# Scaling folded into the value weights, q and k split straight from PSUM, and one-hot lane products moved to ScalarE, in a fused attention and mixture-of-experts kernel

## The reference

```
# 1. self attention over the 1024 pixels of each image
q, k, v = Wq@xf + bq, Wk@xf + bk, Wv@xf + bv          # 32, 32 and 256 rows
y = v @ softmax(q.T @ k, axis=-1).T
x = alpha[0] * y + x
# 2. to tokens (4 x 1024 x 256); proxy attention on the layer norm, with a running sum
prods = proxy @ ln(t).T                               # 16 proxies
y = cumsum(prods[..., None] * ln(t)[:, None], axis=2)
t = t + einsum('bps,bpsd->bsd', softmax(prods / sqrt(16), axis=1), y)
# 3. mixture of 8 experts, top 2 of each token, 256 -> 1024 -> 256
logits = ln(t) @ gate_w.T
combine = one_hot(top2) * softmax(top2 logits)
t = t + sum over e of combine[:, e] * (gelu(ln(t) @ w1[e] + b1[e]) @ w2[e] + b2[e])
```

## Time and profile before

| | |
|---|---|
| time, median of 3 executions | 826.69 us (822.74 to 829.28) |
| the profiled execution | 822.62 us, its span 820.9 us |
| busy PE, DVE, ACT, POOL | 726.5, 500.5, 320.7, 415.4 us |
| mean granted TensorE clock | 0.958 of full speed |

### The profile page before, as it was taken

The page is one execution under the profiler, slowest core; times in us unless marked ns, Lnnn a source line. Parts: engine busy times, 40 slices in busy tenths (PEclk is TensorE's granted clock), DMA queues, the critical chain, the costliest instruction groups (busy, mean ns, idle before and its releaser), DMA issues.

```text
span 820.9 us, 18490 instructions
## 1 busy us (share of the span) xinstructions
PE 726.5 (88%) x5437; PEld 687.8 (84%) x5439; DVE 500.5 (61%) x1095; ACT 320.7 (39%) x608; POOL 415.4 (51%) x480
## 2 busy tenths in 40 slices
PE   5898998988958768637999999999999999999993
PEld 4897897978846556427999999999999999999993
DVE  3787787877774898892545554555545455545551
ACT  2663854735723545223332233223323332332230
POOL 1473574775554454346355564555546555545233
PEclk9999999999988899878999999999999999999998
DMA  7659477494552132222364752756555545554222
GB/s 246 220 196 419 148 269 300 154 326 187 205 206 78 53 105 85 72 79 67 97 188 143 255 150 41 248 154 174 188 177 154 141 144 160 140 145 144 27 28 28
DMA packets 45872, 130.14 MB, mean 159 GB/s; under 512 B 5184, under 2 KB 35520, under 8 KB 41216
## 3 DMA queue, kind: packets, MB, share of 16 engines
q1 hardware_dynamic: 30560, 104.86, 34.1%
q0 software_dynamic: 13904, 19.45, 14.1%
q10 hardware_dynamic: 1360, 5.24, 1.6%
HBM read 186.80 MB, written 47.59 MB: 286 GB/s over the span
## 4 chain that ended last, share of the span: by engine, by line
PE 52%; issue 1%; DMA 1%; POOL 1%; DVE 0%; POOLq 0%; ACT 0%; DVEq 0%
PE ps_h L73 9%; PE ps_h L74 8%; PE ps_h L75 8%; PE ps_y L73 8%; PE ps_y L75 8%; PE ps_y L74 8%; PE ps_x L1585 2%; DMA out_tok<-y,to_row 0%; POOL out_tok L1460 0%; DMA x_rows<-normed,from_row 0%; POOLq L1383 0%; DVE yb L1540 0%; DVE xtl L1520 0%; DVE y L1547 0%; ACT xth L1485 0%
## 5 line engine op out<-in xcount | busy, mean ns | idle before, releaser
L1494 ACT ACTIVATE g<-ps_h,bias 128x256 f32<-128x256 f32 x288 | 120.9, 471 | 278.9 <-PE ps_h L75 278.8
L1460 POOL DMA_INDIRECT out_tok<-y,to_row x72 | 118.3, 1643 | 161.2 <-DVE y L1547 149.4
L73 PE MATMUL ps_h<-xth,wbuf 128*128 128x256 f32 x576 | 163.6, 284 | 3.3 <-issue 1.9
L73 PE MATMUL ps_y<-wbuf,gl 128*128 x576 | 164.4, 285 | 0.0
L74 PE MATMUL ps_h<-xtl,wbuf 128*128 128x256 f32 x576 | 163.5, 284 | 0.0
L75 PE MATMUL ps_h<-xth,wbuf 128*128 128x256 f32 x576 | 162.4, 282 | 0.0
L75 PE MATMUL ps_y<-wbuf,gh 128*128 x576 | 161.4, 280 | 0.0
L74 PE MATMUL ps_y<-wbuf,gh 128*128 x576 | 161.4, 280 | 0.0
L73 PEld LDWEIGHTS ps_h<-xth,wbuf 128*128 128x128 f32 x576 | 108.7, 189 | 3.7 <-issue 2.1
L75 PEld LDWEIGHTS ps_h<-xth,wbuf 128*128 128x128 f32 x576 | 110.1, 191 | 0.0
L74 PEld LDWEIGHTS ps_h<-xtl,wbuf 128*128 128x128 f32 x576 | 108.9, 189 | 0.0
(11 more groups left out here) (239 smaller groups left out, 1391.5 us busy)
## 6 DMA issues: line engine op xcount, KB each, us to landing
wbuf<-wsplit SPq DMA_DIRECT2D x71, 2048.0 KB, 7.4
wsplit<-wbuf SPq DMA_DIRECT2D x14, 2048.0 KB, 11.9
wraw<-in_w SPq DMA_DIRECT2D x16, 1024.0 KB, 7.7
raw<-in_x_ch ACTq DMA_DIRECT2D x5, 1024.0 KB, 9.1
normed<-x SPq DMA_DIRECT2D x8, 528.0 KB, 3.0
tok<-in_x_tok SPq DMA_DIRECT2D x1, 4096.0 KB, 16.7
out_tok<-tok SPq DMA_DIRECT2D x8, 512.0 KB, 3.8
x_rows<-normed,from_row POOLq DMA_INDIRECT x72, 3.3
```

The lines of the kernel that those rows point to most:

```text
L73: eng.matmul(out, ll, rh, start=first, stop=False)
L1460: pool.indirect_dma_start(out=out, out_offset=bass.IndirectOffsetOnAxis(ap=to_row[:, par, s:s + 1], axis=0), in_=y[:, par, s, :], in_offse ...
L1494: last = act.activation(g[:, f, :], ps_h[:, q, f % 2, :], ACT.Gelu_apprx_tanh, bias=bias1[:, bass.ds(e, 1), f:f + 1].rearrange("p a f -> p ...
```

## The change

Alpha is multiplied once, at the start, into v's weights and bias, and the product with alpha for each tile (L558, 32 times) goes. ACT writes the high half of q and k directly from PSUM (`high_qk`), and DVE makes the low half in one instruction from PSUM, bias and high half (`low_qk`); the wait for the last scores of the image before moves to ACT. POOL's subtraction of 128x2048 becomes four of 128x512, with the semaphore on the fourth. In the softmax of the routing weights the subtraction (`relative`) and the last product (`whole_weights`) move from DVE to POOL, and the last image's tiles are cut into batches of 2 and 6 instead of 4 and 4. In stage B the product of lanes and tile number moves from POOL to four activations of 128x256 on ACT (`number_lanes`); POOL's `next_tile` waits for them before it counts up the tile number. PE's `record(i - 2)` stands behind `attend(i + 1)` and `turn(i + 2)`. Some settings to zero are reordered.

```diff
-REST = IT // 2
+EARLY = 2
+PIECES = 4
...
-BATCHES = ((0, NT - 2 * IT), (NT - 2 * IT, NT - IT), (NT - IT, NT - REST), (NT - REST, NT))
+BATCHES = ((0, NT - 2 * IT), (NT - 2 * IT, NT - IT), (NT - IT, NT - IT + EARLY), (NT - IT + EARLY, NT))
...
+    def relative(self, pool, lo, hi, n):
+
+        pool.wait_ge(self.inv_step, n * 6 + 6)
+        pool.wait_ge(self.top_d, n + 1)
+        pool.tensor_tensor(self.weights[:, lo:hi, :], self.t[:, lo:hi, C:C + NP],
+                           self.top[:, lo:hi].unsqueeze(2).to_broadcast([P, hi - lo, NP]), ALU.subtract).then_inc(self.rel_d, 1)
...
+                        if not more and (par, part) == (1, 0):
+                            tok.relative(pool, *BATCHES[2], 2)
...
-                        pool.tensor_tensor(wbuf[:, par, at + n:at + 2 * n], wraw[:, part],
-                                           wbuf[:, par, at:at + n].bitcast(F32), ALU.subtract).then_inc(w_lo, 1)
+                        m = n // PIECES
+                        for i in range(PIECES):
+                            last = pool.tensor_tensor(wbuf[:, par, at + n + i * m:at + n + (i + 1) * m],
...
+                        last.then_inc(w_lo, 1)
...
-            def whole_qk(b, kind):
+            def high_qk(b, kind):
                 act.wait_ge(qk_mm, done(b * 2 + kind))
-                act.wait_ge(turned, done(b * IT - 2 + kind))
-                act.activation(qkf[:, kind], (ps_sc, ps_pt[0])[kind][0:3 * MID, :], ACT.Identity,
-                               bias=bqk[:, kind:kind + 1]).then_inc(qk_full, 1)
+                act.wait_ge(scored, done(b * IT - 1))
+                act.activation(qk3[:, kind], (ps_sc, ps_pt[0])[kind][0:3 * MID, :], ACT.Identity,
+                               bias=bqk[:, kind:kind + 1]).then_inc(qk_hi, 1)
...
-                dve.tensor_copy(qk3[:, kind], qkf[:, kind]).then_inc(qk_hi, 1)
+            def low_qk(b, kind):
+
+                at = slice(MID, 2 * MID) if kind == 0 else slice(2 * MID, 3 * MID)
                 dve.wait_ge(qk_hi, done(b * 2 + kind))
-                at = slice(MID, 2 * MID) if kind == 0 else slice(2 * MID, 3 * MID)
-                dve.tensor_tensor(qk3[at, kind], qkf[at, kind], qk3[at, kind].bitcast(F32), ALU.subtract).then_inc(qk_ok, 1)
+                dve.scalar_tensor_tensor(out=qk3[at, kind], in0=(ps_sc, ps_pt[0])[kind][at, :], scalar=bqk[at, kind:kind + 1],
+                                         in1=qk3[at, kind].bitcast(F32), op0=ALU.add, op1=ALU.subtract).then_inc(qk_ok, 1)
...
-                    dve.tensor_tensor(scale[:, col], scale[:, col], alb[:, :], ALU.mult).then_inc(scaled, 1)
-                    dve.wait_ge(scaled, done(g))
...
-            def lanes_by_tile(c, par):
+            def next_tile(c):
...
+                act.wait_ge(tile_d, done(c - 1))
+                mine = lane[:, :, :].rearrange("p (k b) l -> p b k l", k=2)
+                for b in range(B):
+                    last = act.activation(lane_tile[:, par].rearrange("p (k b) l -> p b k l", k=2)[:, b], mine[:, b], ACT.Copy,
+                                          scale=tile_no[:, b:b + 1])
+                last.then_inc(lane_tile_d, 1)
...
-                if exists(i - 2):
-                    record(i - 2, par)
                 if exists(i + 1):
                     attend(i + 1, 1 - par)
                 if exists(i + 2):
                     turn(i + 2)
+                if exists(i - 2):
+                    record(i - 2, par)
```

More of the change, by code:

```diff
@@ L352, in image @@
                                        ALU.subtract).then_inc(v_ok, 1)
+                static = isinstance(b, int)
+                if not more:
+                    tok.relative(pool, *BATCHES[0], 0)
                 for par in range(2):
@@ L372, in _ @@
         def _(act):
-            for s in (exped, pt_hi, qk_full, v_hi):
+            for s in (exped, pt_hi, qk_hi, v_hi):
                 act.sem_inc(s, CREDIT)
@@ L432, in image @@
                         exp_tile(it + 2)
-                    if not more and it in (REST, IT - 2):
-                        n = 1 + it // (IT - 2)
-                        tok.exponential(act, *BATCHES[n], n)
+                    if not more and it == 1:
+                        tok.exponential(act, *BATCHES[0], 0)
+                    if not more and it == IT - 2:
+                        for n in (1, 2):
+                            tok.exponential(act, *BATCHES[n], n)
                     if it == 2 and more:
@@ L444, in image @@
                 if more:
-                    whole_qk(b + 1, 1)
-                if isinstance(b, int) and b == B - 2:
-                    tok.exponential(act, *BATCHES[0], 0)
+                    high_qk(b + 1, 1)
             load_x(0)
@@ L523, in routing_weights @@
                     if more and it == IT - 2:
-                        tok.softmax_in(dve, *BATCHES[0], 0)
+                        tok.largest(dve, *BATCHES[0], 0)
                     if not more and it == 0:
                         tok.mean_var(dve, *BATCHES[1], 1)
-                        tok.softmax_out(dve, *BATCHES[0], 0)
-                    if not more and it == REST - 1:
-                        tok.softmax_in(dve, *BATCHES[1], 1)
-                    if not more and it == REST:
+                    if not more and it == EARLY:
                         tok.mean_var(dve, *BATCHES[2], 2)
-                    if not more and it == REST + 1:
-                        tok.softmax_out(dve, *BATCHES[1], 1)
-                    if not more and it == IT - 2:
-                        tok.softmax_in(dve, *BATCHES[2], 2)
+                        tok.sums_of_weights(dve, *BATCHES[0], 0)
+                    if not more and it in (3, 5):
+                        n = it // 2
+                        tok.largest(dve, *BATCHES[n], n)
                     if not more and it == IT - 1:
-                        tok.softmax_out(dve, *BATCHES[2], 2)
+                        for n in (1, 2):
+                            tok.sums_of_weights(dve, *BATCHES[n], n)
                 full_v(0)
@@ L894, in body @@
                 if exists(i - 1):
-                    lanes_by_tile(i - 1, 1 - par)
+                    next_tile(i - 1)
             pool.memset(prod_in[:, :, :], 0.0)
@@ L919, in _ @@
             tok.products(pool, fixed, *BATCHES[LAST], LAST)
-            for i in range(-1, 2):
+            body(-1, 1)
+            tok.relative(pool, *BATCHES[LAST], LAST)
+            tok.whole_weights(pool, *BATCHES[LAST], LAST)
+            for i in range(0, 2):
                 body(i, i % 2)
@@ L955, in evacuate_turned, with number_lanes @@
                 last.then_inc(turned_d, 1)
-            def lanes_by_part(c, par):
+            def number_lanes(c, par):
                 act.wait_ge(lane_d, done(c))
@@ L973, in body @@
                 if exists(i - 1):
-                    lanes_by_part(i - 1, 1 - par)
+                    number_lanes(i - 1, 1 - par)
             act.wait_ge(zeroed, 2)
```

101 lines of the change are left out of this document (49 added, 52 removed).

## The result

The changed kernel takes 784.75 us in the median of 4 runs (782.13 to 785.98), against 824.88 us for the kernel before (822.74 to 829.28, 4 runs): a ratio of 0.950, 95% interval 0.945 to 0.955. The forecast for the median was 794.0, the range 779 to 812. The profiled execution took 782.13 us, with a span of 780.4 against 820.9: 40.5 us less, where the sum in the prediction was 32.7.

A forecast was written before the change was run, and what follows sets the result against it. DVE instructions stalled behind long POOL ones, making PE wait in stage A, and the longest ring of engine steps in stage B were taken as bounds; 15.7 + 17.0 = 32.7 us gained, forecast median 794.0 us, range 779 to 812.

The forecast's parts named there:

- Start: Stage A, first image: only an unblocked cast goes, 0.7 of the 1.50 us that PE waits for first scores.
- Image changes: Stage A, three later images: PE's waits for first scores vanish, 8.6 us, and shorter pipeline refills give 3.0 more.
- The refill: Stage A, first scores to first sums after image changes: falls to the first image's 10.18 us, gaining 3.0 together.
- The rival in which the waits stay: Stage A's image changes: ACT's high half queues behind other work, PE waits as before, the 8.6 stay; 803 us, chance 0.07.
- The last image: End of stage A: 3.4 us gained, bounds 1.4 and 5.5, limited by POOL's wait ahead of its last eight pieces.
- the "more is gained" rival: DVE's 9.8 us sets stage B's chunk (4 more) or the last image gives 8.4 (5 more): 785 to 790, chance 0.10.
- Stage B: Five chunks going from 13.39 to 10.6 us give 14.0, the last three chunks 3.0: 17.0 us, bounds 11 and 23.
- the longest ring sets the spacing of the cells: Stage B: of three rings of dependent engine steps, the longest sets the chunk's new period, taken as 10.6 us.
- The ring of ACT and POOL: Stage B chunk: ACT's busy time, four activations and POOL's stretch to ACT's next work make 10.5 us, taken as 10.6.
- its own ring: Stage B chunk on DVE: 13.46 us minus its 1.75 wait for ps_a and about 1.95 of cell stall leaves 9.8.
- The drain: Stage B's last three chunks, where the loop runs out: about 1.0 us gained in each, 3.0 together.
- TensorE's clock: Rival in stage B: PE's granted clock sinks to a mean of 0.6, five chunks lose 4.0 us; 812, chance 0.06.

The follow-up runs named there:

- the late step: Changed kernel with POOL's softmax subtraction of batch 2 between the last two groups of four weight pieces instead of ahead of both: 782.62 us.
- the spread weights: The late step's kernel with ACT's high halves of the weights made one per tile to the end, instead of two at tile 5: 779.94 us.

## Why the prediction was right, and where its sum was off

The direction, the places and most of the mechanisms held. The sum was 7.8 us too small, 3.3 of it in stage A, 3.4 in stage B and the rest outside both. The median, 784.75, lies 9.3 under the forecast; the other 1.5 is the distance from the profiled execution to the median, 2.6 where I added 4.1.

- *Start*, forecast 0.7: the wait fell from 1.50 to 0.84, as worked out. The first sum came 2.0 us earlier: 0.4 more because q's first matmul started at 12.31 instead of 12.71, and 0.9 more because fewer of q's matmuls ran at the lower clock, 0.63 us each (six, eleven before). Among the kernels with the new split, whose PE instructions up to there are the same, the first sum comes between 31.83 and 33.54, so this excess cannot be put down to the change.
- *Image changes*, forecast 8.6 + 3.0: the waits went in full, and the three images gave 13.5. The refill was under-sized, 4.0 for 3.0: from 10.89, 11.63 and 11.45 it falls to 10.05, 9.97 and 9.97, below the first image's 10.18, and the granted clock in these stretches, which was 0.85 and 0.86 at the last two changes before, is 1.00. The forecast of the refill had no term for the clock. The last 1.0 us lies inside the images. The rival in which the waits stay, 803, would have needed ACT to be late; ACT's high half came in time for PE at every change. Of the two causes that I named together, the split alone does it; the pieces are a second remedy for the same wait, and on the kernel before they leave most of it.
- *The last image*, forecast 3.4: 3.5 measured, by the mechanism named, POOL's wait ahead of the last eight pieces. The wait ended at 208.42 in a stage whose last image began 15.5 us earlier than before (at 180.98 against 196.48), so at 223.9 by the old clock, where I had 224.5. The 8.4 that the "more is gained" rival allowed was there to take: the late step and the spread weights take 4.4 more.
- *Stage B*, forecast 14.0 + 3.0: here a step failed, that the longest ring sets the spacing of the cells. The ring of ACT and POOL, for which I had 10.6, was sized nearly right: ACT's normalisations, released by POOL, follow at 10.19 to 10.56. But DVE's cells do not wait for it. Three of the five blocks follow at 9.88 or 9.89 and one at 9.99, with no wait of DVE: its own ring, which I had put at 9.8 and among the rivals at 0.10 (785 to 790; the median lies at its edge). ACT's lanes fall behind, from 0.12 to 1.26 us after the first cell, and catch up where the loop runs out. The remaining chunk takes 10.70, and its limit is PE, busy for all of it behind a chunk at a clock of 0.83; DVE waits 0.70 for `ps_out`. In the run with the weights spread the chunk ahead is at 1.00 and DVE waits nowhere. Whether the longer ring would set the pace of a longer loop, no run shows.

```profile
265.17:275.87 10.70, 10.70 (x62) 8.31 (x60) 9.80 (x58) 8.71 (x22) 4.98 (x19) 1.00 0.29 100
...
267.52 0.19 DVE L1025 TENSOR_TENSOR raw_logit<-ps_out,tok 128x32 f32<-128x32 f32 x1 [0.70 <-PE ps_out L1270]
...
270.80 2.08 ACT L944 ACTIVATE raw<-tok,inv_shift 128x256 f32 x4 [1.06 <-POOL inv_shift L847]
...
281.36 2.08 ACT L944 ACTIVATE raw<-tok,inv_shift 128x256 f32 x4 [1.12 <-POOL inv_shift L847]
...
291.54 2.08 ACT L944 ACTIVATE raw<-tok,inv_shift 128x256 f32 x4 [0.98 <-POOL inv_shift L847]
```

The terms: the four activations take 1.69, not 1.9, and from the lanes' end to ACT's next normalisation it is 2.08 to 2.46 us, where I had 2.2; eight free cells take 1.67, not 1.4. Five chunks gave 16.6. The drain and the table gave 3.9; I had 3.0.

- *Rivals*: TensorE's clock did not sink: four of the five chunks run at 1.00, the first at 0.83. Four strided activations cost 0.49 us each (1.97 for all in a sum of single durations, 1.69 as they overlap), far from the 1.6 at which the kernel would have been slower.

The rule that I weighed, multiplications on VectorE rather than ScalarE, would have put the lanes on DVE, the engine that is back to back in the chunk: at least 0.7 us more on a ring of 9.88, by the prediction's estimate. That was not run; what the runs show is that DVE's cells did not wait for ACT, though its turns are the longer ones.

## What to carry to other kernels

A row whose mean is far above its free duration (0.70 against 0.15 us for one column) points at an instruction of another engine that holds it up, but it says nothing about what that costs: alpha's row (15 us beside the new split) was worth about 1 us there, while the 28 us of q's and k's cast and subtraction were worth 12.6 beside whole POOL instructions, and 2.7 beside pieces. Look where the stalled instruction has a waiter. Two remedies for the same wait do not add (the operand in PSUM, the shorter piece), and two waits in a row on one ring can give more together than one by one (3.3 us for 0.9 and 1.7), so test them in pairs. A step that is moved to an idle engine is put behind everything that the engine must release early: ask what stands behind its wait there.

## What the runs showed of the hardware that was not expected

- The hold works in both directions. Beside DVE's casts and subtractions of q and k, with their operands in SBUF, POOL's four pieces took 7.56 us instead of 5.04; the whole instruction, begun during a cast, took 5.08 instead of 4.61.
- One operand in PSUM frees a DVE instruction wholly: 1.28 us at all eight places, six of them beside a POOL subtraction.
- The pieces cost POOL little: four took 4.95 to 5.07 us where the one took 4.58 to 4.63.
